# Projection steps placed by a table in the attention stage, and the accumulators copied by one instruction behind two score chunks

## The reference, cut to what matters

```python
xn = layernorm(x)                                   # x: 4 x 4096 x 1024
def attn(xn):                                       # 16 heads of 64
    Q, K, V = (xn @ W + b for each of Wq, Wk, Wv)   # split into heads
    attn = softmax(einsum('bhqd,bhkd->bhqk', Q, K) / sqrt(64))
    out = relu(einsum('bhqk,bhkd->bhqd', attn, V) @ Wo + bo)
    return (out - mean(out)) * rsqrt(var(out) + 1e-5)
def ffn(xn):                                        # one of 8 experts for a token
    e = argmax(xn @ Wr.T)
    y = gelu(xn @ W1[e] + b1[e]) @ Wo2 + bo2 + xn   # 1024 -> 4096 -> 1024
    return (y - mean(y)) * rsqrt(var(y) + 1e-12) * gamma + beta
result = x + attn(xn) + ffn(xn)
```

## Time and profile before

| What | us |
|---|---|
| Time, median of three runs (lowest, highest) | 1857.01 (1852.81, 2019.57) |
| Time of the profiled execution | 1858.14 |
| Span of its slowest core, core 1, whose trace is shown | 1856.6 |
| Spans of the eight cores | 1843.0 to 1856.6 |
| First exponential of attention starts | 147.34 |
| Last run of exponentials (27 of them) starts; it lasts 27.23 | 1219.04 |

### The profile page before, as it was taken

One profiled execution on the slowest core, in us unless ns is written; L12 is line 12 of the kernel. 1 busy time (PEld: TensorE's weight loads), 2 busy tenths in 40 slices (PEclk: granted clock), 3 DMA queues, 4 the chain that ended last, 5 costly groups with the idle time before them and its releaser, 6 DMA issues.

```text
span 1856.6 us, 43286 instructions; the slowest of 8 cores (1843.0 to 1856.6 us)
## 1 busy us (share of the span) xinstructions
PE 1672.6 (90%) x15784; PEld 945.0 (51%) x15784; DVE 730.6 (39%) x1348; ACT 1352.4 (73%) x1540; POOL 322.5 (17%) x357
## 2 busy tenths in 40 slices
PE   3778998999999999999999997879699999999995
PEld 2554554454554454554554553334466666666652
DVE  4762453452452453443443544228203233323133
ACT  4878998999999999999999999986433332233210
POOL 1110000001000000000000000001222344533335
PEclk8999999999999999999999999999899999999998
DMA  8984445336455435445444446735866766666622
GB/s 203 265 214 75 70 70 85 71 70 98 81 93 86 69 70 92 73 72 86 70 70 69 70 81 148 170 70 192 285 215 199 230 205 215 216 213 205 223 75 95
DMA packets 54207, 244.05 MB, mean 131 GB/s; under 512 B 8176, under 2 KB 8816, under 8 KB 51696
## 3 DMA queue, kind: packets, MB, share of 16 engines
q0 software_dynamic: 25056, 137.91, 36.3%
q1 hardware_dynamic: 28368, 102.84, 17.3%
q10 hardware_dynamic: 576, 0.45, 0.1%
HBM read 295.69 MB, written 105.91 MB: 216 GB/s over the span
## 4 chain that ended last, share of the span: by engine, by line
PE 81%; issue 6%; DVE 5%; ACT 3%; DMA 2%; POOL 1%; another core or an unknown queue 0%; DVEq 0%; ACTq 0%; POOLq 0%; SPq 0%
PE acc L910 24%; PE sc L899 14%; PE zp L700 14%; PE yp L713 11%; PE fb L802 8%; PE fb L807 5%; PE yp L988 3%; PE fb L817 1%; DVE stA L1402 1%; DVE stB L1403 1%; DMA stB<-wr_c 1%; ACT xnT L1112 1%; DMA xg<-xseq,idxg 1%; ACT P L1129 1%; ACT xnb L1095 1%
## 5 line engine op out<-in xcount | busy, mean ns | idle before, releaser
L1129 ACT ACTIVATE P<-sc,negm 128x1024 bf16<-128x1024 f32 x1024 | 1061.9, 1125 | 37.1 <-PE sc L899 31.9
L910 PE MATMUL acc<-P,V 64*128 64x512 bf16 x4096 | 627.1, 377 | 29.8 <-DVE stB L1403 29.2
L899 PE MATMUL sc<-QT,KT 64*128 64x512 bf16 x2048 | 405.2, 379 | 49.4 <-issue 29.5
L700 PE MATMUL zp<-xeT,w1r 128*128 128x288 bf16 x2048 | 294.3, 290 | 15.1 <-ACT hT L1035 15.0
L1035 ACT ACTIVATE hT<-zp,small 128x288 bf16<-128x288 f32 (+2 forms) x256 | 119.9, 470 | 249.3 <-PE zp L700 233.1
L910 PEld LDWEIGHTS acc<-P,V 64*128 64x128 bf16 x4096 | 224.7, 94 | 133.5 <-issue 56.4
L713 PE MATMUL yp<-wo,hT 128*128 128x512 bf16 x1088 | 271.5, 379 | 0.0
L899 PEld LDWEIGHTS sc<-QT,KT 64*128 64x128 bf16 x2048 | 123.2, 93 | 268.5 <-issue 237.3
L700 PEld LDWEIGHTS zp<-xeT,w1r 128*128 128x128 bf16 x2048 | 202.4, 99 | 111.4 <-issue 16.5
L625 POOL DMA_DIRECT2D w1bf<-w_c x128 | 63.0, 493 | 899.2 <-ACT P L1129 899.2
L802 PE MATMUL fb<-xnT,wqkv 64*128 64x512 bf16 x1344 | 215.5, 378 | 3.2 <-DVE KT L1251 0.6
(11 more groups left out here) (149 smaller groups left out, 1192.9 us busy)
## 6 DMA issues: line engine op xcount, KB each, us to landing
w1bf<-w_c POOLq DMA_DIRECT2D x128, 512.0 KB, 5.6
w1r<-w1bf SPq DMA_DIRECT2D x128, 512.0 KB
xt<-xseq SPq DMA_DIRECT2D x32, 512.0 KB, 6.7
xb_scr<-xnf POOLq DMA_DIRECT2D x16, 512.0 KB, 7.5
wo2bf<-wo_c POOLq DMA_DIRECT2D x16, 512.0 KB, 5.7
wo<-wo2bf SPq DMA_DIRECT2D x16, 512.0 KB, 5.7
res_scr<-rt SPq DMA_DIRECT2D x16, 512.0 KB, 3.9
xn_scr<-xnf POOLq DMA_DIRECT2D x16, 256.0 KB, 6.8
```

The lines of the kernel that those rows point to most:

```text
L700: ins = te.matmul(zp[z % 2][:, 0:CAP], w1r[k % 8][:, kc * 256 + (ic % 2) * 128:kc * 256 + (ic % 2 + 1) * 128], xeT[:, kc * XR + lo:kc * XR ...
L899: ins = te.matmul(sc[n % 2][:, h * 512:(h + 1) * 512], KT[g % 2][h * 64:(h + 1) * 64, c * 128:(c + 1) * 128], QT[g % 2][h * 64:(h + 1) * 6 ...
L910: return te.matmul(acc[h][:, :], V[(n // 128) % 2][lo:lo + 64, c * 192 + h * 64:c * 192 + h * 64 + 128], P[n % 6][lo:lo + 64, h * 512:(h + ...
L1129: se.activation(out=P[n % 6][:, :], in_=sc[n % 2][:, :], func=AF.Exp, bias=negm[g % 2][:, :], scale=0.125).then_inc(s_P, 1)
```

## The change

Three things change, all in the attention stage.

```diff
 def fill_plan(g):
...
-    rate = 1.0
-    while not spread(rate)[1]:
-        rate += 0.01
-    return spread(rate)[0]
+    plan, at = [], 0
+    for n in range(128):
+        k = int(STEPS[0 if g == 0 else 1][n])
+        plan.append(runs[at:at + k])
+        at += k
+    assert at == len(runs)
+    return plan
...
+                fresh = a >= 0 and a % 32 == 0 and a > 0
                 if n + 2 < 1024:
                     te.wait_ge(s_P, n + 1)
                     scores(n + 2)
+                if fresh:
+
+                    for two, part, phase, u in plan[0]:
+                        step(g + 1, two, part, phase, u)
+                    te.wait_ge(s_P, n + 2)
+                    scores(n + 3)
+                    for two, part, phase, u in plan[1]:
+                        step(g + 1, two, part, phase, u)
+                    te.wait_ge(s_cp, a // 32)
                 if a >= 0:
...
-                    if a % 32 == 0 and a > 0:
-
-                        for two, part, phase, u in plan[0]:
-                            step(g + 1, two, part, phase, u)
-                        plan[0] = []
-                        te.wait_ge(s_cp, 2 * (a // 32))
...
-                for two, part, phase, u in plan[0]:
-                    step(g + 1, two, part, phase, u)
-                if n + 3 < 1024:
-                    te.wait_ge(s_P, n + 2)
-                    scores(n + 3)
+                if not fresh:
+                    for two, part, phase, u in plan[0]:
+                        step(g + 1, two, part, phase, u)
+                    if n + 3 < 1024:
+                        te.wait_ge(s_P, n + 2)
+                        scores(n + 3)
...
-                for two, part, phase, u in plan[1]:
-                    step(g + 1, two, part, phase, u)
+                if not fresh:
+                    for two, part, phase, u in plan[1]:
+                        step(g + 1, two, part, phase, u)
...
-                ve.tensor_copy(out=stA[:, :], in_=acc[0][:, :]).then_inc(s_cp, 1)
-                ve.tensor_copy(out=stB[:, :], in_=acc[1][:, :]).then_inc(s_cp, 1)
+                ve.tensor_copy(out=stAB[:, :], in_=accAB[:, :]).then_inc(s_cp, 1)
```

More of the change, by code:

```diff
@@ L75, in n_steps @@
     return {"Q": 8, "K": 8, "V": 2}.get(kind, 1)
+STEPS = (
+    "2222122111022222222012221221120112222222021122222201221222220221"
+    "1222220110110022222112201101102112222220011011022222112201111000",
+    "2222121211022222212102222122210222221122011222222202121222220222"
+    "1122220110011011222202220110110020202022211201100110221122222000")
 def fill_plan(g):
@@ L225, in build @@
         st_w = ExitStack()
-        stA = sb(st_w, "stA", 512, F32)
-        stB = sb(st_w, "stB", 512, F32)
+        stAB = sb(st_w, "stAB", 1024, F32)
+        stA, stB = stAB[:, 0:512], stAB[:, 512:1024]
         lsb = [stA[:, j * 128:(j + 1) * 128] for j in range(2)]
@@ L301, in build @@
         sc = [ps(pa, f"sc{j}", 1024, F32) for j in range(2)]
-        acc = [ps(pa, f"acc{j}", 512, F32) for j in range(2)]
+        accAB = ps(pa, "accAB", 1024, F32)
+        acc = [accAB[:, 0:512], accAB[:, 512:1024]]
         fb = [ps(pa, f"fb{j}", 512, F32) for j in range(2)]
@@ L978, in _ @@
             te.wait_ge(s_E, n_ve)
-            te.wait_ge(s_cp, 64)
+            te.wait_ge(s_cp, 32)
             for tt in range(16):
@@ L1408, in divide @@
                 if step == 0:
-                    ve.wait_ge(s_cp, 2 * q + 2)
+                    ve.wait_ge(s_cp, q + 1)
                     ve.tensor_copy(out=sums[0:64, :], in_=stA[64:128, :])
```

## The result

The changed kernel takes 1846.5 us (median of 8 runs), the kernel before 1857.0 in the same session. The ratio is 0.9947, with a 95% interval from 0.9936 to 0.9958: 9.8 us less, between 8 and 12. In a 2% sense nothing changed; the interval says that the gain is real. Executions in which a die's clock was lowered for long are left out of the ratios, and of the times in the table of the experiments.

A forecast was written before the change was run, and what follows sets the result against it. The prediction took ScalarE's exponentials to bound attention, losing time when TensorE is over 0.14 us late. Order and copy 9.6, table 3.5 and 0.1, less 1.6 for routing, make 11.6 off 1857.0: 1845.4 us, range 1839 to 1852.

The forecast's parts named there:

- ScalarE's rhythm: Attention: exponentials at 1.005 us a chunk set its end; TensorE may be 0.14 us late before ScalarE loses time.
- Order and copy: Attention's group boundaries: new order and merged copy save 1.2 us a later group, 9.6 us over eight groups.
- the ledger: Attention: running sum of TensorE's lateness, chunk cost less 1.005 us, never below zero; anything over 0.14 is lost to ScalarE.
- The copy: VectorE at boundaries: one double-width copy takes 1.23 us where two took 1.29, 0.06 less.
- The wait between the halves: TensorE at a boundary: it stands 0.33 us for `s_X` between first and second value halves.
- the slower rival: Boundaries: value halves wait longer than the copy did, 0.62 us more each, giving 1865 us; chance 0.10.
- The table: Attention's step placement: the new table saves 0.7 us in each of five later groups, 3.5, and 0.1 in the first.
- The routing work: Second group: `RT` complete two chunks later lengthens the stall, costing 1.6 us, 1.1 in the ledger and 0.5 for the clock.
- The stages behind attention: After attention: what follows starts earlier by the same amount as attention saves; no DMA is moved past another.
- The signs named ahead: Attention: idle one exponential later, 0.4 to 0.7; later group 134.3 to 135.0; last quarters 32.5; routing stall some 8 us.
- nothing moves: First 70 chunks of a group: TensorE is full, so boundary gains may be lost again; 1857 us, chance 0.17.
- The boundaries vanish: The 31 boundaries: copy wholly hidden, eight values absorbed, 0.65 to 0.75 us back each, some 22, giving 1833; chance 0.13.

The follow-up runs named there:

- e6: e4 with TensorE's waits for exponentials left out where an earlier wait already covers them; 1823.8 us, ratio 0.9834 to the kernel before.
- e7: e4 with one more wait for an already reached count ahead of each pair of scores; 1847.3 us, ratio 0.9944 to the kernel before.
- e1: The changed kernel with the old step table, keeping the new boundary order and single copy; 1849.5 us, ratio 0.9999 to the kernel before.
- e3: The kernel before with only the two copies merged into one of twice the width; 1852.7 us, ratio 1.0008.
- e2: The kernel before with only the new step table, keeping two copies and the old boundary order; 1852.3 us, ratio 1.0008.
- e10: e9 with the old step table; 1822.1 us, ratio 0.9804 to the kernel before.
- e5: The kernel before with the routing instructions cut in three parts at chunks 8, 18 and 28 of the second group; 1847.9 us, ratio 0.9956.
- e4: The changed kernel with the routing instructions cut in three parts, behind the accumulators' copy in the second group; 1832.9 us, ratio 0.9893 to the kernel before.
- e8: e4 with the scores of the chunk after next placed between the value halves at a boundary; 1834.1 us, ratio 0.9880 to the kernel before.
- e9: The changed kernel with routing parts later, repeated waits left out and scores between the halves at a boundary; 1816.9 us, ratio 0.9769 to the kernel before.

## Why the prediction was right

The forecast was 11.6 us less, 1845.4; measured are 9.8 by the ratio, 10.5 by the medians, 10.1 in attention. By its steps:

- **ScalarE's rhythm bounds the stage, and TensorE's lateness beyond 0.14 is what it loses.** Right, and shown from both sides by e6 and e7. The 31.9 us of visible waits were not the measure of the gain: after the change they are 33.4, and the time fell all the same.
- **Order and copy, 9.6 us.** The mechanism is right, the term too large. e1 gives 0.9 a later group where the ledger had 1.2, and the last group, which has no steps and so no table, fell by 0.8 (130.6 to 129.8) and not 1.2. What I had left out is that the waits of TensorE ahead of the first halves stand in a row, and that the change put `s_cp` at its front. In the new order they are `s_cp` and `s_P`, in the first boundary of a group `s_E` too, and each one behind `s_cp` takes 0.1 after the copy is done. Here is such a boundary, the first of the fourth group:

```profile
572.04 1.23 DVE L1403 COPY stAB<-accAB 128x1024 f32<-128x1024 f32 x1 [3.74 <-PE accAB L905]
...
572.63 0.39 PE L894 MATMUL sc<-QT,KT 64*128 64x512 bf16 x2
...
572.84 0.61 PE L797 MATMUL fb<-xnT,wqkv 64*128 64x512 bf16 x4
...
573.63 1.36 PE L905 MATMUL accAB<-P,V 64*128 64x512 bf16 x8 [0.17 <-issue]
...
575.30 3.12 ACT L1130 ACTIVATE P<-sc,negm 128x1024 bf16<-128x1024 f32 x3 [0.92 <-PE sc L894]
```

The copy ends at 573.27, the first halves start at 573.63, 0.36 later, where my 0.15 was from the old order, whose waits for `s_P` and `s_E` were already through. ScalarE is idle for 0.92 here, 0.35 of it because the copy itself started late (572.04 for values that ended at 571.52; elsewhere that distance is 0.17).

e6 tests this reading, since it leaves the wait for `s_P` out of that row. Its boundary of n = 482, where `s_cp` stands alone:

```profile
654.81 1.23 DVE L1404 COPY stAB<-accAB 128x1024 f32<-128x1024 f32 x1 [1.26 <-PE accAB L905]
...
656.18 1.36 PE L905 MATMUL accAB<-P,V 64*128 64x512 bf16 x8
```

The copy ends at 656.04 and the values start 0.14 later, where it was 0.26; at the first boundary of the fourth group it is 0.25, where it was 0.36. So the lag is 0.15, 0.25 and 0.36 with one, two and three waits. Boundaries with two steps, where the copy is done in time, came out as laid out: from scores n+3 to n+4 it is mostly 1.83 to 1.85 (1.84 forecast). At n = 482 the scores n+4 come 2.71 behind n+2 and not 2.57, 0.11 of it by this wait. In e1 the copy ends last at the first and the second boundary of a later group, with lags of 0.36 and 0.25, and at those of the last group, with 0.25. That is some 0.2 of the 0.3 that a later group of e1 lacks, and 0.3 of the 0.4 that the last group lacks; the rest was not traced.

- **The copy.** 1.22 to 1.23, as laid out. Alone (e3) it brought somewhat more than the 2 us of its term.
- **The wait between the halves, 0.33.** Right: eight matmuls take 1.36, from 573.63, where it would be 1.04 without (0.61 for four, 0.43 for four more). This was what the slower rival hung on; it would have had to be 0.63.
- **The table, 3.5 us in five groups.** 0.85 a group instead of 0.7 (e2), 0.8 in e10.
- **The routing work, 1.6.** Between 1.4 and 2.1 (e5 against e4). Its part for the clock, 0.5, is in the rows: the scores behind the stall start 1.99 after the values where 1.19 is normal, and in the old order 0.81 where 0.43 is; 0.80 less 0.38 is 0.42.
- **The stages behind attention** neither gave back nor added: by the median of the cores what follows it takes 603.3 where it took 603.8. On core 1 alone, attention starts 2.1 later, takes 8.4 less (its third group has 139.0, those of the others 135.0 to 137.1), and what follows it takes 606.7 where it took 610.3. Such differences of 2 to 4 us outside attention are of the size of those between cores.
- **The signs named ahead.** The idle moved one exponential later, the routing stall is 8.48 (some 8), and the 0.3 before the second halves is there. Three came out a little off. A later group takes 135.25, where 134.3 to 135.0 was forecast: the ledger was already low for the kernel before (136.2, and 137.1 is the mean), so its differences were better than its values. The last group's quarters are 32.68, not 32.5. The idle of ScalarE at a boundary is mostly 0.4 to 0.6, but 0.73 at the first one of the third and the fifth group and 0.92 at that of the fourth (0.4 to 0.7 forecast).

Of the rivals, "nothing moves" is excluded by the interval, whose upper end is 0.9958. "The boundaries vanish" did not happen; the reason given, two score buffers, was not tested by more of them, and in e8 and e9, where 0.3 is left at a boundary, it is the buffers of `P` that hold ScalarE. "Slower" hung on the wait between the halves, which is 0.33. The forecast is 1.5 us above what attention gave. The boundary was too good by some 2.5 and the table too poor by some 0.7, so the total is closer than its largest term: that part is luck.

## What to carry to other kernels

Where an engine is fed through two buffers, write down how late the feeding engine may be before the fed one waits (here 0.14 us of 1.0), and carry that slack through the order of work; sums of waits show neither the loss nor the gain (31.9 before, 33.4 after, for 10.1 us less). A wait for a count that is already reached is not free where its engine has nothing queued behind it to work on: leaving out repeated ones took 9.9 us off a stage of 1079. Where several waits stand in a row, put the one that is reached last at the end: with `s_cp` at the front, each wait behind it came on top (that order, changed alone, was not run). And look once at every long chain that is the only one of its kind: 12 us of small VectorE instructions ahead of a copy that others wait for cost 9.0, nearly as much as the whole change brought.

## What the runs showed of the hardware that I had not expected

Each further wait instruction of TensorE for a count already reached moved the start of the scores by 0.1 us: 1.27, 1.38 and 1.47 from the exponential's start with one, two and three waits. Behind the copy it is the same, 0.15, 0.25 and 0.36.

In e1 the granted clock of two cores was 0.81 for a long stretch behind the routing stall, neither of the two levels. Core 7, between 310 and 320 us:

```profile
310.00:320.00 10.00, 9.97 (x78) 4.46 (x76) 2.28 (x4) 8.76 (x9) 0.49 (x1) 0.81 0.29 54
```

and core 0 in the same execution and window:

```profile
310.00:320.00 10.00, 9.80 (x92) 4.98 (x89) 2.28 (x4) 9.91 (x11) 0.49 (x1) 1.00 0.30 55
```

78 matmuls against 92 and 9 exponentials against 11. The second group took 158.3 and 158.4 on cores 6 and 7 and 141.6 to 143.9 on the others. On core 7 the stretch lasts from 301 to 462 us. e2 (cores 6 and 7) and e3 (cores 0 and 1) have the same one, 160 to 161 us long, always in two neighbouring cores while the other two of their die stay at 1.00. In e8, which has no routing stall, cores 4 and 5 had it from 155 to 317, right behind the start of attention, so the stall is not its only cause. In all four it began 4 to 7 us after a stretch at 1.2 GHz had ended. What sets it off stays open.

The distance from the last values to the start of the copy was 0.17 at nearly all boundaries and 0.52 at two (before) or one (changed), the same ones on all cores. Which ones goes by the number of copy instructions alone: the 6th and the 24th boundary in the three kernels with two copies (before, e2, e5), the 12th in the nine with one, whatever the order, the table or the routing work. Why is open.
